# Causal attention weighed for four heads at once, in pieces of four key blocks, in place of two heads over whole rows

## The reference

```
T, C = 2048, 512;  H, HKV, HD = 16, 4, 128          # G = 4 query heads share one key head
q, k, v = rope(x @ Wq + bq), rope(x @ Wk + bk), x @ Wv + bv
scores = einsum('bgjtd,bjsd->bgjts', q, k) / sqrt(H)
scores = where(tril, scores, -inf)                   # causal: query block b sees key blocks 0..b
out = einsum('bgjts,bjsd->bgjtd', softmax(scores), v)
x = layernorm(x + out @ Wo + bo)
```

## Time and profile before

| | us |
|---|---|
| median of 3 runs (lowest to highest) | 2105.62 (2104.97 to 2106.53) |
| the profiled execution | 2106.28 |
| its span in the trace | 2104.5 |
| PE busy | 2071.4 |
| DVE busy | 1677.3 |
| ACT busy | 1395.6 |
| POOL busy | 862.4 |

### The profile page before, as it was taken

One profiled execution on the slowest core, in us unless ns is written; L12 is line 12 of the kernel. 1 busy time (PEld: TensorE's weight loads), 2 busy tenths in 40 slices (PEclk: granted clock), 3 DMA queues, 4 the chain that ended last, 5 costly groups with the idle time before them and its releaser, 6 DMA issues.

```text
span 2104.5 us, 39565 instructions
## 1 busy us (share of the span) xinstructions
PE 2071.4 (98%) x13609; PEld 1843.9 (88%) x13609; DVE 1677.3 (80%) x3567; ACT 1395.6 (66%) x2790; POOL 862.4 (41%) x813
## 2 busy tenths in 40 slices
PE   9999999999999999999999999999989999999998
PEld 8888878999889998899988999988878999999996
DVE  6899987888678876788767887666667889898886
ACT  3677766766667666676656766533446777777775
POOL 1000013333233332333323333245556777778874
PEclk9999999999999999999999999999999999999999
DMA  8558563210331103311053110478648999999998
GB/s 267 184 211 288 213 215 118 71 61 21 130 122 71 61 21 126 126 69 63 21 185 126 66 66 21 150 258 287 240 138 240 299 295 302 297 293 298 296 289 261
DMA packets 139636, 361.28 MB, mean 172 GB/s; under 512 B 16337, under 2 KB 33233, under 8 KB 134865
## 3 DMA queue, kind: packets, MB, share of 16 engines
q1 hardware_dynamic: 111376, 292.03, 39.6%
q0 software_dynamic: 28096, 67.12, 13.4%
HBM read 224.21 MB, written 134.89 MB: 171 GB/s over the span
## 4 chain that ended last, share of the span: by engine, by line
PE 80%; ACT 2%; DMA 2%; DVE 2%; issue 1%; POOL 0%; DVEq 0%; ACTq 0%; SPq 0%; POOLq 0%
PE p_S L690 18%; PE p_O L725 17%; PE p_TP L702 11%; PE p_pgu L1538 9%; PE p_acc L1080 9%; PE p_prest L1538 4%; PE p_py L1555 4%; PE p_tp L1524 3%; PE p_py L1556 1%; PE p_py L1557 1%; ACT p_prob L771 1%; DMA o_scratch<-p_oT 1%; PE p_lg L1102 1%; DMA qk_scratch<-p_qout 1%; ACT p_pT1h L780 0%
## 5 line engine op out<-in xcount | busy, mean ns | idle before, releaser
L690 PE MATMUL p_S<-p_kT,p_q 128*128 128x512 f32 (+3 forms) x1920 | 472.5, 376 | 10.2 <-ACT p_prob L771 9.6
L886 POOL TENSOR_SCALAR p_prob<-p_prob,p_inv 128x128 f32<-128x128 f32 (+7 forms) x256 | 191.3, 747 | 453.4 <-DVE p_inv L835 453.4
L690 PEld LDWEIGHTS p_S<-p_kT,p_q 128*128 128x128 f32 x1920 | 322.5, 189 | 61.2 <-ACT p_prob L771 17.1
L886 POOL TENSOR_SCALAR p_prob<-p_prob,p_inv,p_part 128x1024 f32<-128x1024 f32 x128 | 153.2, 1197 | 483.2 <-DVE p_inv L840 483.2
L702 PE MATMUL p_TP<-p_ident,p_prob 128*128 128x128 f32 x2176 | 303.1, 274 | 2.5 <-DVE p_pT1l L846 2.1
L702 PEld LDWEIGHTS p_TP<-p_ident,p_prob 128*128 128x128 f32 x2176 | 244.2, 140 | 31.0 <-issue 18.0
L824 DVE TENSOR_REDUCE p_nmax<-p_S 128x1 f32<-128x1024 f32 (+7 forms) x256 | 253.2, 989 | 20.7 <-PE p_S L690 15.1
L780 ACT CAST p_pT0h<-p_TP 128x512 fp32r<-128x512 f32 (+3 forms) x320 | 155.0, 527 | 134.1 <-PE p_TP L702 133.7
L780 ACT CAST p_pT1h<-p_TP 128x512 fp32r<-128x512 f32 (+3 forms) x320 | 154.8, 526 | 128.7 <-PE p_TP L702 128.1
L1812 POOL DMA_INDIRECT sum_scratch<-p_y,p_tokT x124 | 207.5, 1674 | 42.6 <-issue 37.2
L725 PE MATMUL p_O<-p_pT0h,p_v 128*128 128x256 f32 x1088 | 222.7, 288 | 0.2 <-DVE p_pT0l L846 0.2
(11 more groups left out here) (351 smaller groups left out, 4665.8 us busy)
## 6 DMA issues: line engine op xcount, KB each, us to landing
p_w_raw<-in_gu SPq DMA_DIRECT2D x64, 768.0 KB
qk_scratch<-p_qout SPq DMA_DIRECT2D x80, 512.0 KB, 2.8
p_q<-qk_scratch SPq DMA_DIRECT2D x16, 2048.0 KB, 9.4
o_scratch<-p_oT SPq DMA_DIRECT2D x128, 256.0 KB, 2.2
p_ot<-o_scratch SPq DMA_DIRECT2D x32, 1024.0 KB, 7.3
p_w_raw<-in_gu SPq DMA_DIRECT2D x64, 256.0 KB
v_scratch<-p_vout SPq DMA_DIRECT2D x16, 512.0 KB, 3.2
p_t_raw<-in_dn SPq DMA_DIRECT2D x32, 256.0 KB
```

The costliest lines, as they stand in the source:

```text
L690: mm = nc.tensor.matmul(out, x, y, start=(n == 0), stop=(n == 2))
L886: nc.gpsimd.tensor_scalar(prob[k][:, cols], prob[k][:, cols], inv[:, k:k + 1], scale, ALU.mult, ALU.mult).then_inc(normed, 1)
```

## The change

- Weighing is by fours: the four heads of a query block stand side by side, so O is 128 x 512 (a whole PSUM bank) and each matmul is 512 wide. There are half as many.
- pT holds 4 key blocks for 4 heads (a piece), twice. A four with n key blocks has ceil(n/4) pieces (`PIECE`, `in_piece`), turned piece by piece over all four heads. `turns(i)` puts the four's turns into steps 4f+5 to 4f+8, as many in each as it has pieces.
- `weigh_behind(m, g)` puts one key block of the former piece m-1 behind each turn of piece m; where the former piece has fewer than 4 blocks, the first heads' turns have none behind them.
- In a wide step the two score groups surround two turns, and the weighings behind these two come after the second group (`wide_step`).
- out_hi and out_lo work on 512 columns, 64 times in place of 128, at the end of a step and of the next. `store` sends four heads at once; the loads of k, v and q hang on other stores.
- KEEP is 8. The loop over key heads is one loop over 256 units.

```diff
-    KEEP = 5
-    LAG = 3
-    WEIGH = LAG + 2
-    OUT = WEIGH + 2
+    KEEP = 8
+    TURN = 5
+    FREE = 2
+    STEPS = ALL + TURN
...
+    def turns(i):
+        if i < TURN:
+            return []
+        f, k = divmod(i - TURN, G)
+        n = npieces(f)
+        return [(PG[f] + r // G, r % G) for r in range(k * n, (k + 1) * n)]
...
+        return f * G + TURN + G + (3 // npieces(f + 1) if f + 1 < QUADS else 0)
...
-        pT = [[sb(f"pT{k}{s}", [P, NB, 2, P], F32R) for s in "hl"] for k in range(2)]
-        oT = [sb(f"oT{k}", [P, 2, 2, P], F32R) for k in range(2)]
+        pT = [[sb(f"pT{k}{s}", [P, 4, G, P], F32R) for s in "hl"] for k in range(2)]
+        oT = [sb(f"oT{k}", [P, G, 2, P], F32R) for k in range(2)]
...
-        O = [ps(f"O{k}", [P, 2, P]) for k in range(2)]
+        O = [ps(f"O{k}", [P, G, P]) for k in range(2)]
...
+            def turn(m, g):
+                f, t = PIECE[m]
+                u = f * G + g
+                pe.wait_ge(normed, SG[u] + t // 2 + 1)
+                pe.wait_ge(turn_lo, m * G + g + 1)
+                for n in range(in_piece(m)):
+                    s = 4 * t + n
+                    mm = nc.tensor.transpose(TP[g % 2][:, n, :], prob[u % KEEP][:, s * P:(s + 1) * P], ident[:])
...
+                if n == 0:
+                    pe.wait_ge(turn_lo, m * G + G + FREE)
+                for i, (x, y) in enumerate(split3([v[:, s, h, :] for h in (HI, LO)],
+                                                  [pT[m % 2][h][:, n, :, :] for h in (HI, LO)])):
+                    mm = nc.tensor.matmul(O[f % 2][:], x, y, start=(s == 0 and i == 0),
...
+            def weigh_behind(m, g):
+                n = g - (G - in_piece(m - 1)) if m > 0 else -1
+                if n >= 0:
+                    weigh(m - 1, n)
...
+            def wide_step(i, one, two, *others):
+                scores(i, 0)
+                turn(*one)
+                if two[1] == 0:
+                    weigh_behind(*one)
+                turn(*two)
+                scores(i, 1)
+                if two[1] > 0:
+                    weigh_behind(*one)
+                weigh_behind(*two)
+                for at in others:
+                    turn_and_weigh(*at)
...
-                at = lagged(i, OUT, first)
-                if at and i % 2 == OUT % 2:
-                    out_hi(j, at[1], at[0] // 2, first)
...
+                if i in OUT:
+                    out_hi(OUT[i])
```

More of the change, by code:

```diff
@@ L589, in load_v @@
                          .rearrange("b o p h d -> (o p) b h d")).then_inc(v_in[c], 16)
[L591 to L604, removed]
         def first_k(sp):
@@ L694, in scores @@
                 mm.then_inc(scored, 1)
[L696 to L702, removed]
-                mm.then_inc(turned, 1)
@@ L705, in weigh @@
[L705 to L712, removed]
-                        pe.wait_ge(v_in0, 16)
[L714 to L730, removed]
@@ new lines, in step @@
+            def step(i):
+                todo = turns(i)
+                if i < ALL and ngrp(i) == 2:
+                    wide_step(i, *todo)
+                    return
+                ahead = 2 if len(todo) == 4 else 0
+                for at in todo[:ahead]:
+                    turn_and_weigh(*at)
+                if i < ALL:
+                    scores(i, 0)
+                if i == 1:
+                    keep_busy(nc, 20, S[:, 0, 512:512 + P], ident[:])
+                for at in todo[ahead:]:
+                    turn_and_weigh(*at)
@@ L782, in out_hi @@
-            def out_hi(j, back, p, first):
-                act.wait_ge(weighed, j * PAIRS + (p + 1 + FREE - back * PAIRS))
-                if not (first and p < 2):
-                    act.wait_ge(o_out[p % 2], j * (8 * PAIRS) + (16 * (p // 2) - back * 8 * PAIRS))
-                nc.scalar.copy(oT[p % 2][:, :, HI, :], O[p % 2][:]).then_inc(o_hi, 1)
-            def step(j, i, first):
-                at = lagged(i, OUT, first)
-                if at and i % 2 == OUT % 2:
-                    out_hi(j, at[1], at[0] // 2, first)
-                at = lagged(i, LAG, first)
-                turns = [(j, at[1], at[0], t) for t in range(ntr(at[0]))] if at and i < U + LAG else []
-                for a in range(2):
-                    for args in turns[2 * a:2 * a + 2]:
-                        p_hi(*args)
-                    if i < U and a < ngrp(i):
-                        exp(j, i, a)
@@ new lines, in step @@
+            def step(i):
+                todo = turns(i) if i < STEPS else []
+                for a in range(2):
+                    for m, g in todo[2 * a:2 * a + 2]:
+                        p_hi(m, g)
+                    if i < ALL and a < ngrp(i):
+                        exp(i, a)
+                if i in OUT:
+                    out_hi(OUT[i])
+            for i in range(LAST):
+                step(i)
+                if ALL < i <= ALL + len(between):
+                    between[i - ALL - 1](act)
@@ new lines, in step @@
+            def step(i):
+                if i % U == 0 and 0 < i < ALL:
+                    take_k(i // U)
+                if i % U == TURN - 1 and U < i < ALL:
+                    take_v(i // U)
+                todo = turns(i) if i < STEPS else []
+                if i < ALL:
+                    row_max(i, 0)
+                if 1 <= i <= ALL:
+                    recip(i - 1)
+                for m, g in todo[0:2]:
+                    p_lo(m, g)
+                if i < ALL and ngrp(i) == 2:
+                    row_max(i, 1)
+                for m, g in todo[2:]:
+                    p_lo(m, g)
+                if i - 1 in OUT:
+                    out_lo(OUT[i - 1])
@@ L878, in gpsimd @@
+            for i in range(LAST + 1):
+                step(i)
+                if ALL + 1 < i <= ALL + 1 + len(between):
+                    between[i - ALL - 2](dve)
         def gpsimd(pool):
```

226 lines of the change are left out of this document (105 added, 121 removed).

## The result

The changed kernel takes 2134.56 us (median of 4 runs, 2132.57 to 2136.93) where the kernel before takes 2106.07: a ratio of 1.0137 (1.0124 to 1.0150). It is slower by 28.5 us; 2100.8 was forecast and 2114 was the end of the range. The profiled execution took 2132.57, 26.3 more than that of before. In this text the kernel after the change is "after".

What follows compares the result with a forecast made beforehand. PE's queue was taken to set the end. Terms -11.9 + 7.6 + 1.6 - 3.6 + 1.5 = -4.8 us on the profiled 2106.28 gave 2101.5, hence a forecast median of 2100.8 us, range 2089 to 2114.

Steps and rivals of the forecast that it cites:

- Longer lag, more prob buffers: At heads' starts, turns come later and ACT and DVE take out less: 3.6 us gained, bounds 0 to 8.
- uneven steps: Wide steps whose first turns have few or no weighings behind them fall under 4.36 us: 7.6 us lost, bounds 2 and 14.
- the end: Attention's end: last weighing waits for cast and subtraction, output-weight pieces stand between subtractions: 1.5 us lost, bounds 0 and 4.
- Weighings 512 wide: PE's weighings in the attention: 3264 become 1632 at 0.2323 us instead of 0.1198 each, 11.9 us saved.
- Narrow steps of 5 and 6 blocks: First step of either four: PE has only scores and two turns, less than DVE's work: 1.6 us lost, bounds 0 and 3.
- Waits added: Each turn waits for its own unit's normalisation, loads hang on other stores: costed at nothing.
- The late exp: Four-turn wide steps: second scores wait for group 1's exp behind a cast; 16 to 19 us slower, 2118; chance 0.19.
- The pace by columns: A 512-wide weighing takes nearly twice a 256-wide one: 0 to 4 us saved, 7.1 lost, about 2110; chance 0.06.
- the skill's rule: Matmul distance on PE of N/2.4 + 2.5 ns: two made one save 2.6 ns, 4.2 us in all, as an estimate.

Runs made afterwards that it cites:

- the last run: Scores ahead of turns in narrow four-turn steps, evenly cut pieces, and of two pieces the smaller first, against the kernel before: 2101.34 us, ratio 0.9977.
- Two missed experiments: Three-block pieces weighed behind turns 0, 1, 2 instead of 1, 2, 3: on the changed kernel 2137.5 us; with scores first in narrow four-turn steps 2115.1.

## Why the prediction was wrong

- **"Longer lag, more prob buffers" is the step that failed.** It put a gain of 3.6 us at the heads' starts, bounds 0 to 8, from shorter waits for exp. The seams lost 23.4 instead. I had priced the lag alone. The steps at a seam have four turns and narrow scores. In them PE makes two turns ahead of the scores while DVE has the maximum ahead of the subtractions, and that was so before. What the change took away is the run of weighings between the scores and the third turn, which had covered the subtractions' lateness; I put that at nothing. This term is 27.0 of the 32.3 us between the forecast sum and the attention's growth. The two runs that undo the order on either side give back 19.5 and 19.3 us; what is left then is still 0.4% slower than before, mostly through the uneven steps and the end, two terms further down that were too small. With the order mended the seams still lose 2.9 more than before, so the gain of 3.6 is not to be seen there.
- **Weighings 512 wide: right.** 11.9 forecast; 12.2 as worked out from the paces above, 0.233 each in the chain. Undone, 8.9 to 10.9.
- **Uneven steps: right in kind and place, too small.** 7.6 forecast, bounds 2 and 14. The blocks of 9 to 12 lose 14.0 more and those of 13 to 15 2.2 less: 11.8. Units 33 and 41 lose 1.11 and 1.14 (1.0 and 1.15 forecast). Unit 45 loses 0.94 where 0.3 was said, and units 38, 39, 42 and 46, of which nothing was said, lose 0.3 to 0.6 each. Per head that makes 6.7 us where 4.0 was counted; for the kernel before 2.1 was counted and it is 3.2. The floor of 4.36 was confirmed by the last run. Two missed experiments show that a weighing from the neighbouring short step only moves the stall; it took work from outside the run of short steps.
- **Narrow steps of 5 and 6 blocks:** 1.6 forecast; these blocks lose under 0.2 a head before and after. Wrong, and small.
- **The end:** 1.5 forecast, bounds 0 and 4; 4.5 measured, outside them. The last piece's weighings start 0.86 late (0.8 forecast). The rest is mostly eight waits of 0.2 to 0.55 ahead of turns and weighings in the steps without scores, and of those the forecast had 0.7. What causes them stays open.
- **Waits added:** nothing forecast, and right: the steps of 13 to 16 blocks have no wait of that kind.
- **The rivals.** The late exp was the only one well on the slower side, and its reason isn't what happened: the four-turn wide steps lose less than before, not 0.25 us more each. The pace by columns is refuted by the weighings' distance. I had no rival in which PE's and DVE's queues are in different orders. In the paragraph on the skill's rule, 2.6 ns and 4.2 us come from rounded distances; the rule gives 2.5 ns and 4.1 us, and nothing else hangs on it.

The forecast's own terms with the measured sizes: -12.2 + 11.8 + 0 + 23.4 + 4.5 = 27.5, which is the attention's growth; the profiled execution grew by 26.3.

## What to carry to other kernels

When a change reorders one engine, lay each step's order on the engines that feed each other side by side, at every kind of step, the rare ones too: an instruction that waits in a queue holds back finished work behind it, and what hid that before may be the work that was moved. A step that a round trip holds to a fixed length, as those of 4.36 us here, takes more work at no cost and gives no time back for less; so cut pieces evenly and put the surplus there. In this kernel a wait that only moved when its neighbour was reordered was the sign of such a step. And not every long row of waits is a loss: the wide maximum's 90 us stayed while 19.5 us were won.

## What the runs showed of the hardware

Nothing in the chip's behaviour was new against the rows of before; the surprises were of order. One number was firmer than expected: a weighing of 512 columns, with its own weights loaded, keeps 0.233 us in runs of 3 between transposes (0.70 for three in the chain of after). Two of 256 columns made one saved 5.5 to 6.7 ns there, so that gain needs no long run of products.
